# One-head attention: three fp16 passes for scores and values, turning two tiles behind, ScalarE's copies ahead of the exponential

## The chip, the cores and the metric

The kernel runs on one NeuronCore of a Trainium2 chip. Engines: TensorE (PE) with its weight loads (PEld), VectorE (DVE), ScalarE (ACT), GpSimd (POOL) and SyncE (SP). The metric is the time of one execution on the device in microseconds, the median of several runs.

## The reference

The whole program is a model of four layers, each of them an attention and a feed-forward part. The change touches the second branch of layer 0, a softmax attention with one head over x normalised, shape 4 x 1024 x 128, in fp32:

```python
q = x @ Wq + bq
k = x @ Wk + bk
v = x @ Wv + bv
scores = jnp.einsum('bqh,bkh->bqk', q, k) / sqrt(128)
attn = softmax(scores, axis=-1)
a = jnp.einsum('bqk,bkh->bqh', attn, v) @ Wo + bo
x = x + a
```

Its result goes into a softmax router and eight dense experts, the stages behind it. There are 4 batches of 1024 rows.

## The kernel before

`whole_attention` (L876) is called once, as stage `b0`; its tiles carry the prefix b_ in the profile. Data lie with the 128 features on the partitions. The work is cut into 32 tiles of 128 query rows, 8 per batch (`qts`); each tile's scores are 128 x 1024.

Five instruction streams are written out, one per engine, and every one walks the same list of jobs, `order`, made by `timeline()` (L884); semaphores join them. A step s of the list is: scores of tile s, turning of tile s-1, values of tile s-2; in the steps 4, 5 and 6 of a batch also k, q and v of the next batch; and every fourth step a projection with 512 columns. The jobs:

- k, q (L959): fp32 matmuls into one of the two wide PSUM buffers (`wide_ps`, 1024 columns each, shared with the scores). ScalarE adds k's bias (L1003), VectorE q's bias and scale (L1034).
- v (L966): eight fp32 matmuls into the PSUM tile `turned`, copied by ScalarE (L1014).
- scores (L974): two fp32 products with 512 columns into a wide buffer. VectorE takes the row maximum (L1042) and negates it (L1044), ScalarE makes exponential and row sum (L1008), VectorE the reciprocal (L1026) and scales the row (L1028), which is `normalise`.
- turn (L981): eight fp32 transposes of 128 x 128 of the scaled tile into `turned`, which has one buffer; ScalarE copies it to `prob_t` (L1019).
- values (L988): eight fp32 products of 128 columns into a quarter of `mix`. After four tiles VectorE adds v's bias (L1051, `mixed`).
- proj (L995): product with the output weights; VectorE adds bias and residual into `xp_t` (L1055), GpSimd adds that into `res_t` (L1063).

An fp32 product appears as two matmul records in the profile. VectorE runs `normalise(n - 1)` ahead of the row maximum of tile n. A wide buffer is refilled when its reader two slots before has freed it (`wait_freed`):

```python
if slot[job] >= 2:
    wait_freed(eng, wide[slot[job] - 2])
```

## Time and profile before

| | us |
|---|---|
| median of 3 runs | 4607.53 |
| lowest, highest run | 4606.55, 4609.24 |
| the profiled execution | 4609.92 |
| its span | 4608.0 |

Busy over the whole span:

| engine | busy us | share |
|---|---|---|
| PE | 4038.5 | 88% |
| PEld | 2252.7 | 49% |
| DVE | 3471.0 | 75% |
| ACT | 2976.9 | 65% |
| POOL | 2359.2 | 51% |

The profile is of one execution. Busy shares are means over stages that differ, so the stage of the change has to be looked at by itself. Matmuls are pipelined: a record's length is longer than the distance between two starts, and the distance is what it costs. The names "out<-in" are the program's tiles, and L numbers are lines of the kernel before.

### The profile page before, as it was taken

To read this page: it belongs to the slowest core of one execution; us is meant where nothing else is said; L and a number is where in the kernel's file an instruction comes from. 1 tells how busy PE (TensorE), PEld (TensorE's weight loads), DVE (VectorE), ACT (ScalarE), POOL (GpSimd) and SP (SyncE) were. 2 spreads that over 40 slices of the span, in tenths; PEclk is the share of its full clock that TensorE was granted. 3 is DMA by queue.
4 is the path that set the end of the run, shared out by engine and by line. 5 is a ranking of instruction groups with operands and counts; after the bars stand their busy time and mean duration, and the time that the engine had idled before them with its cause. 6 is when DMAs were issued, how large, how long until landed. Compare 5 with 4: busy or idle time off the path is not lost. (4 is left out here: it accounts for less than half of the span.)

```text
span 4608.0 us, 88475 instructions
## 1 busy us (share of the span) xinstructions
PE 4038.5 (88%) x34698; PEld 2252.7 (49%) x34700; DVE 3471.0 (75%) x4781; ACT 2976.9 (65%) x4498; POOL 2359.2 (51%) x1443
## 2 busy tenths in 40 slices
PE   6999999999998989976787778886888868999998
PEld 3666666666666644441121111434777443344443
DVE  6888888888884567756989897564777647988888
ACT  2777777777775469943767777672665725655555
POOL 2878887888883023320221110451666526666665
PEclk7999999999999989976989999997999979999999
DMA  2212221222110011100210100430000223333433
GB/s 81 57 43 53 57 55 45 51 57 57 45 41 1 1 70 69 46 5 25 81 62 27 39 26 6 128 125 19 13 13 14 100 91 98 88 101 99 99 96 87
DMA packets 112123, 261.46 MB, mean 57 GB/s; under 512 B 24020, under 2 KB 35668, under 8 KB 110236
## 3 DMA queue, kind: packets, MB, share of 16 engines
q1 hardware_dynamic: 96292, 215.01, 17.0%
q0 software_dynamic: 15424, 40.89, 2.6%
q8 instruction: 271, 4.44, 0.4%
q14 instruction: 136, 1.11, 0.1%
HBM read 170.31 MB, written 49.76 MB: 48 GB/s over the span
## 5 line engine op out<-in xcount | busy, mean ns | idle before, releaser
L522 POOL TENSOR_TENSOR a_prob_low<-a_prob_whole,a_prob_high 128x1024 f16<-128x1024 f32 x512 | 1084.4, 2131 | 277.2 <-ACT a_prob_high L412 275.4
L496 DVE TENSOR_REDUCE a_part_max<-a_top 128x2 f32<-128x1024 f32 x512 | 626.1, 1223 | 218.7 <-PE a_top L323 212.8
L409 ACT ACTIVATE a_prob_whole<-a_score 128x1024 f32<-128x1024 f32 x512 | 524.9, 1025 | 332.5 <-PE a_score L312 320.6
L767 ACT ACTIVATE a_prob<-a_score 128x512 f32<-128x512 f32 x1024 | 533.1, 604 | 259.3 <-PE a_score L711 259.2
L799 DVE TENSOR_REDUCE a_part_max<-a_side 128x2 f32<-128x1024 f32 x512 | 595.0, 1218 | 83.7 <-PE a_side L682 83.7
L1943 POOL TENSOR_TENSOR m_scaled<-m_acted,m_gate 128x512 f32<-128x512 f32 x264 | 433.3, 1650 | 269.4 <-DVE m_acted L2061 200.7
L412 ACT ACTIVATE a_prob_high<-a_score 128x1024 f16<-128x1024 f32 x512 | 522.3, 1020 | 0.0
L311 PE MATMUL a_score<-a_qa,a_ka 128*128 128x256 f16 x2048 | 476.3, 273 | 0.0
L312 PE MATMUL a_score<-a_qb,a_kb 128*128 128x256 f16 x2048 | 476.2, 273 | 0.0
L378 PE MATMUL a_o_ps<-a_v,a_prob_high 128*128 128x65 f16 x4096 | 428.1, 193 | 6.2 <-POOL a_prob_low L522 3.4
L380 PE MATMUL a_o_ps<-a_v,a_prob_high 128*128 128x64 f16 x4096 | 426.9, 194 | 0.0
L382 PE MATMUL a_o_ps<-a_v,a_prob_low 128*128 128x65 f16 x4096 | 424.5, 192 | 0.0
L378 PEld LDWEIGHTS a_o_ps<-a_v,a_prob_high 128*128 128x128 f16 x4096 | 376.0, 96 | 85.7 <-DVE a_tokens L482 35.3
L380 PEld LDWEIGHTS a_o_ps<-a_v,a_prob_high 128*128 128x128 f16 x4096 | 377.7, 97 | 26.9 <-issue 10.9
L382 PEld LDWEIGHTS a_o_ps<-a_v,a_prob_low 128*128 128x128 f16 x4096 | 377.9, 98 | 0.0
L1894 ACT ACTIVATE m_acted<-m_up_down 128x512 f32<-128x512 f32 x264 | 157.4, 597 | 319.4 <-PE m_up_down L1723 318.7
L711 PE MATMUL a_score<-a_qa,a_ka 32*128 32x512 f16 x1024 | 237.2, 398 | 91.0 <-ACT a_prob L767 88.6
L723 PE MATMUL a_o_ps<-a_prob,a_v 128*32 128x512 f32 x2048 | 285.9, 632 | 14.0 <-ACT a_raw L756 14.0
L2280 DVE TENSOR_TENSOR e_low<-e_whole,e_high 128x512 f16<-128x512 f32 x256 | 210.5, 833 | 82.7 <-ACT e_high L2238 82.1
L711 PEld LDWEIGHTS a_score<-a_qa,a_ka 32*128 32x128 f16 x1024 | 60.4, 92 | 431.1 <-ACT a_prob L767 366.6
L682 PE MATMUL a_side<-a_ka,a_qa 32*128 32x512 f16 x1024 | 217.4, 403 | 45.3 <-DVE a_part_max L799 22.6
L2067 DVE TENSOR_TENSOR m_lows<-m_scaled,m_high 128x512 f16<-128x512 f32 x264 | 241.8, 916 | 5.1 <-ACT m_high L1902 5.0
(439 smaller groups left out, 10380.4 us busy)
## 6 DMA issues: line engine op xcount, KB each, us to landing
m_gate<-gates SPq DMA_DIRECT2D x264, 256.0 KB
a_ka<-a_nat_high_k SPq DMA_DIRECT2D x128, 128.0 KB, 2.4
e_gate<-gates SPq DMA_DIRECT2D x8, 2048.0 KB, 7.2
slots<-in_slots SPq DMA_DIRECT2D x19, 520.0 KB, 4.1
a_qa<-a_nat_high_q SPq DMA_DIRECT2D x64, 128.0 KB, 2.4
a_qa<-a_nat_low_q SPq DMA_DIRECT2D x64, 128.0 KB, 2.4
a_qb<-a_nat_high_q SPq DMA_DIRECT2D x64, 128.0 KB, 2.4
a_kb<-a_nat_low_k SPq DMA_DIRECT2D x64, 128.0 KB, 2.4
```

Source lines behind the costliest of these rows:

```text
L311: eng.matmul(score[:, e % 2, h, i, :], ka[:, r, h, keys], qa[:, r, h, qs], start=True, stop=False)
L312: mm = eng.matmul(score[:, e % 2, h, i, :], kb[:, r, h, keys], qb[:, r, h, qs], start=False, stop=True)
L378: eng.matmul(o_ps[:, at:at + V1], high, v[:, r, kt, h, 0:V1], start=(pair == 0 and i == 0 and h == 0 and t == 0), stop=False, skip_group_c ...
L380: eng.matmul(o_ps[:, at:at + DH], high, v[:, r, kt, h, V1 + 1:VW], start=False, stop=False, skip_group_check=True)
L382: mm = eng.matmul(o_ps[:, at:at + V1], low, v[:, r, kt, h, 0:V1], start=False, stop=last, skip_group_check=True)
L409: eng.activation(prob_whole[:, e % RING, :, :, :], score[:, e % 2, :, :, :], ACT.Exp, scale=scale)
L412: eng.activation(prob_high[:, e % RING, :, :, :], score[:, e % 2, :, :, :], ACT.Exp, scale=scale).then_inc(exp_done, 1)
L496: eng.tensor_reduce(part_max[:, i, c, :, qt % 4], top[:, :, :], AX.X, ALU.max).then_inc(max_done, 1)
L522: eng.tensor_tensor(prob_low[:, e % RING, :, :, :], prob_whole[:, e % RING, :, :, :], prob_high[:, e % RING, :, :, :], ALU.subtract).then_ ...
L767: eng.activation(prob[:, e % RING, h, :], score[:, step % SLOTS, :], ACT.Exp).then_inc(exp_done, 1)
L799: op = eng.tensor_reduce(part_max[:, qt // 4, c, 2 * pair:2 * pair + 2, 24 + qt], side, AX.X, ALU.max)
L1943: eng.tensor_tensor(scaled[:, s % SR, :], acted[:, s % AR, :], gate[:, g % 2, j, c % 2 * BANK:(c % 2 + 1) * BANK], ALU.mult).then_inc(scal ...
```

## The change

1. k, q, v and the turned probabilities are each split in two fp16 parts: high is the value rounded to fp16, low the rest. Scores and values become three fp16 products (high x high, high x low, low x high), each with fp32 accumulation. The projections and the transposes stay fp32.
2. The high parts are made by ScalarE, the low parts of v and the turned tiles by VectorE (value in PSUM minus high), those of k and q by GpSimd. k and q are now first written in fp32 to one buffer each, then split.
3. `turned` is handled in two halves of 512 columns, each with waits of its own. Its fp16 parts are kept for four tiles side by side, so that values take 512 columns at once: the eight key tiles of a group of four query tiles are shared out over four value jobs, two each.
4. Turning runs two tiles behind the scores (before: one), values six (before: two, by tile), projections three steps later.
5. VectorE takes the row maximum of tile s, then the low parts of tile s-2, then scales tile s-1. ScalarE copies the high parts of tile s-2 ahead of the exponential of tile s.

The diff, cut:

```diff
+    HALF = qts // 2
...
-        for s in range(tiles + 3):
+        for s in range(tiles + 7):
             b, t = s // qts, s % qts
             if s < tiles:
                 order.append(("scores", s))
-            if 1 <= s < tiles + 1:
-                order.append(("turn", s - 1))
             if 2 <= s < tiles + 2:
-                order.append(("values", s - 2))
+                order.append(("turn", s - 2))
+            if 6 <= s < tiles + 6:
+                order.append(("values", s - 6))
             if b + 1 < B and t in (4, 5, 6):
                 order.append(("kqv"[t - 4], b + 1))
-            if s >= 3 and (s - 3) % 4 == 3:
-                order.append(("proj", (s - 3) // 4))
+            if s >= 10 and (s - 10) % 4 == 0:
+                order.append(("proj", (s - 10) // 4))
...
+    act_order = list(order)
+    for s in range(2, tiles):
+        i = act_order.index(("scores", s))
+        act_order[i:i + 2] = [("turn", s - 2), ("scores", s)]
...
-    turns = [job for job in order if job[0] in ("v", "turn")]
+    turns = [(*job, h) for job in order if job[0] in ("v", "turn") for h in range(2)]
...
-        q = pl.sb("q", [P, 2, N])
-        k = pl.sb("k", [P, 2, N])
-        v = pl.sb("v", [P, 2, qts, P])
+        q = pl.sb("q", [P, N])
+        k = pl.sb("k", [P, N])
+        q_high = pl.sb("q_high", [P, 2, N], F16)
+        q_low = pl.sb("q_low", [P, 2, N], F16)
+        k_high = pl.sb("k_high", [P, 2, N], F16)
+        k_low = pl.sb("k_low", [P, 2, N], F16)
+        v_high = pl.sb("v_high", [P, 2, qts, P], F16)
+        v_low = pl.sb("v_low", [P, 2, qts, P], F16)
...
-        prob_t = pl.sb("prob_t", [P, 2, N])
+        prob_high = pl.sb("prob_high", [P, 2, qts, BANK], F16)
+        prob_low = pl.sb("prob_low", [P, 2, qts, BANK], F16)
...
-        turned = pl.ps("turned", [P, N])
+        turned = pl.ps("turned", [P, 2, HALF, P])
...
+        def parts_of(what, n, h):
+            kts = slice(h * HALF, (h + 1) * HALF)
+            if what == "v":
+                return v_high[:, n % 2, kts, :], v_low[:, n % 2, kts, :]
+            at = slice(n % 4 * P, (n % 4 + 1) * P)
+            return prob_high[:, n // 4 % 2, kts, at], prob_low[:, n // 4 % 2, kts, at]
...
+                def product(dst, highs, lows, first, last):
+                    eng.matmul(dst, highs[0], highs[1], start=first, stop=False)
+                    eng.matmul(dst, highs[0], lows[1], start=False, stop=False)
+                    return eng.matmul(dst, lows[0], highs[1], start=False, stop=last)
...
+                    elif what in ("v", "turn"):
+                        if what == "turn":
+                            eng.wait_ge(prob_ready, n + 1)
+                        for h in range(2):
+                            i = turn[what, n, h]
+                            if i >= 2:
+                                eng.wait_ge(turned_read, i - 1)
+                            for t in range(HALF):
+                                kt = h * HALF + t
+                                if what == "v":
+                                    mm = eng.matmul(turned[:, h, t, :], xn_t[:, n * N + kt * P:n * N + (kt + 1) * P], w[:, 2, :], start=True, stop=True)
+                                else:
+                                    mm = eng.transpose(turned[:, h, t, :], prob[:, n % 3, kt * P:(kt + 1) * P], ident[:, :])
+                            mm.then_inc(turned_full, 1)
...
                         if t == 0:
-                            wait_freed(eng, ("k", b))
-                            wait_freed(eng, ("q", b))
+                            eng.wait_ge(qk_split, 2 * (b + 1))
+                        here = slice(t * P, (t + 1) * P)
                         for h in range(2):
-                            mm = eng.matmul(dst[:, h * BANK:(h + 1) * BANK], q[:, b % 2, t * P:(t + 1) * P],
-                                            k[:, b % 2, h * BANK:(h + 1) * BANK], start=True, stop=True)
+                            at = slice(h * BANK, (h + 1) * BANK)
+                            mm = product(dst[:, at], (q_high[:, b % 2, here], k_high[:, b % 2, at]), (q_low[:, b % 2, here], k_low[:, b % 2, at]), True, True)
...
                     elif what == "values":
-                        eng.wait_ge(turned_read, turn["turn", n] + 1)
-                        if n % 4 == 0 and n:
-                            eng.wait_ge(mixed_half, n // 4)
-                        for kt in range(qts):
-                            mm = eng.matmul(mix[:, t % 4 * P:(t % 4 + 1) * P], v[:, b % 2, kt, :], prob_t[:, n % 2, kt * P:(kt + 1) * P],
-                                            start=(kt == 0), stop=(kt == qts - 1))
-                        mm.then_inc(mixed_tile, 1)
+                        m, i = n // 4, n % 4
+                        if i == 0:
+                            eng.wait_ge(turned_read, turn["turn", 4 * m + 3, 1] + 1)
+                            if m:
+                                eng.wait_ge(mixed_half, m)
+                        for kt in (2 * i, 2 * i + 1):
+                            mm = product(mix[:, :], (v_high[:, b % 2, kt, :], prob_high[:, m % 2, kt, :]),
+                                         (v_low[:, b % 2, kt, :], prob_low[:, m % 2, kt, :]), kt == 0, kt == qts - 1)
+                        mm.then_inc(mixed_part, 1)
...
-                for job in by_act:
+                for job in act_order:
...
                     if what == "k":
                         eng.wait_ge(wide_full, slot[job] + 1)
-                        eng.activation(k[:, n % 2, :], wide_ps[:, slot[job] % 2, :], ACT.Identity, bias=bias[:, 1:2]).then_inc(act_freed, 1)
+                        if n:
+                            eng.wait_ge(qk_split, 2 * n - 1)
+                        eng.activation(k[:, :], wide_ps[:, slot[job] % 2, :], ACT.Identity, bias=bias[:, 1:2]).then_inc(act_freed, 1)
+                        wait_freed(eng, job)
+                        eng.activation(k_high[:, n % 2, :], k[:, :], ACT.Copy).then_inc(qk_high_done, 1)
+                    elif what == "q":
+                        wait_freed(eng, job)
+                        eng.activation(q_high[:, n % 2, :], q[:, :], ACT.Copy).then_inc(qk_high_done, 1)
...
                         if n >= 3:
-                            eng.wait_ge(turned_full, turn["turn", n - 3] + 1)
+                            eng.wait_ge(turned_full, turn["turn", n - 3, 1] + 1)
...
+                    elif what in ("v", "turn"):
+                        if what == "v" and n >= 2:
+                            eng.wait_ge(mixed_part, qts * (n - 1))
+                        if what == "turn" and n >= 8:
+                            eng.wait_ge(mixed_part, 4 * (n // 4 - 1))
+                        for h in range(2):
+                            eng.wait_ge(turned_full, turn[what, n, h] + 1)
+                            eng.activation(parts_of(what, n, h)[0], turned[:, h, :, :], ACT.Copy).then_inc(turned_high, 1)
...
                     if what == "q":
                         eng.wait_ge(wide_full, slot[job] + 1)
-                        eng.tensor_scalar(q[:, n % 2, :], wide_ps[:, slot[job] % 2, :], bias[:, 0:1], scale, ALU.add, ALU.mult).then_inc(dve_freed, 1)
+                        if n:
+                            eng.wait_ge(qk_split, 2 * n)
+                        eng.tensor_scalar(q[:, :], wide_ps[:, slot[job] % 2, :], bias[:, 0:1], scale, ALU.add, ALU.mult).then_inc(dve_freed, 1)
                     elif what == "scores":
-                        if n:
-                            normalise(n - 1)
                         eng.wait_ge(wide_full, slot[job] + 1)
                         at = slice(n % 4, n % 4 + 1)
                         if n >= 4:
-                            wait_freed(eng, ("scores", n - 4))
+                            eng.wait_ge(prob_ready, n - 3)
                         eng.tensor_reduce(top[:, at], wide_ps[:, slot[job] % 2, :], AX.X, ALU.max).then_inc(maxed, 1)
                         eng.wait_ge(maxed, n + 1)
                         eng.tensor_scalar(top[:, at], top[:, at], -1.0, None, ALU.mult).then_inc(negated, 1)
-                    elif what == "turn" and n == tiles - 1:
-                        normalise(n)
+                        if n == 1:
+                            normalise(0)
+                    elif what in ("v", "turn"):
+                        for h in range(2):
+                            i = turn[what, n, h]
+                            highs, lows = parts_of(what, n, h)
+                            eng.wait_ge(turned_high, i + 1)
+                            eng.tensor_tensor(lows, turned[:, h, :, :], highs, ALU.subtract).then_inc(turned_read, 1)
+                        if what == "turn" and n + 1 < tiles:
+                            normalise(n + 1)
...
-                for n in range(tiles // 4):
-                    at = slice(n * BANK, (n + 1) * BANK)
-                    eng.wait_ge(xp_done, n + 1)
-                    eng.tensor_tensor(res_t[:, at], res_t[:, at], xp_t[:, at], ALU.add).then_inc(res_done, 1)
+                splits = 0
+                for job in order:
+                    what, n = job
+                    if what in ("k", "q"):
+                        splits += 1
+                        whole, highs, lows = (k, k_high, k_low) if what == "k" else (q, q_high, q_low)
+                        eng.wait_ge(qk_high_done, splits)
+                        eng.tensor_tensor(lows[:, n % 2, :], whole[:, :], highs[:, n % 2, :], ALU.subtract).then_inc(qk_split, 1)
+                    elif what == "proj":
+                        at = slice(n * BANK, (n + 1) * BANK)
+                        eng.wait_ge(xp_done, n + 1)
+                        eng.tensor_tensor(res_t[:, at], res_t[:, at], xp_t[:, at], ALU.add).then_inc(res_done, 1)
```

**TensorE.** Rows of the order of instructions, in the middle of a batch; wide is the wide buffer, turned the transposed tile, mix the value sums. Before, from turning of one tile to the values of the next:

```order
L981 MATMUL b_turned<-all_kept_ident,b_prob 128x128 x8
L988 MATMUL b_mix<-b_prob_t,b_v 128x128 x8
L974 MATMUL b_wide<-b_k,b_q 128x512 x2
L981 MATMUL b_turned<-all_kept_ident,b_prob 128x128 x8
L988 MATMUL b_mix<-b_prob_t,b_v 128x128 x8
```

And now, from turning of one tile to the end of the next scores:

```order
L999 MATMUL b_turned<-all_kept_ident,b_prob 128x128 x8
L971 MATMUL b_mix<-b_prob_high,b_v_high 128x512
L972 MATMUL b_mix<-b_prob_low,b_v_high 128x512
L973 MATMUL b_mix<-b_prob_high,b_v_low 128x512
L971 MATMUL b_mix<-b_prob_high,b_v_high 128x512
L972 MATMUL b_mix<-b_prob_low,b_v_high 128x512
L973 MATMUL b_mix<-b_prob_high,b_v_low 128x512
L971 MATMUL b_wide<-b_k_high,b_q_high 128x512
L972 MATMUL b_wide<-b_k_low,b_q_high 128x512
L973 MATMUL b_wide<-b_k_high,b_q_low 128x512
```

The order of the kinds is the same; turning is that of a tile one older, and values are six products for a group of four tiles.

**VectorE**, the same place: maximum, negation, then scaling. Before:

```order
L1042 TENSOR_REDUCE b_top<-b_wide 128x1
L1044 TENSOR_SCALAR b_top<-b_top 128x1
L1026 RECIPROCAL b_total<-b_total 128x1
L1028 TENSOR_SCALAR b_prob<-b_prob,b_total 128x1024
L1042 TENSOR_REDUCE b_top<-b_wide 128x1
```

Now:

```order
L1075 TENSOR_REDUCE b_top<-b_wide 128x1
L1077 TENSOR_SCALAR b_top<-b_top 128x1
L1085 TENSOR_TENSOR b_prob_low<-b_turned,b_prob_high 128x4x128 x2
L1059 RECIPROCAL b_total<-b_total 128x1
L1061 TENSOR_SCALAR b_prob<-b_prob,b_total 128x1024
```

Two subtractions stand between the negation and the scaling, and the scaling is that of the tile before.

**ScalarE**, around k of the next batch. Before, each tile's exponential stands ahead of the copy of the tile before it:

```order
L1003 ACTIVATE b_k<-b_wide,all_kept_bias_b 128x1024
L1008 ACTIVATE b_prob,b_total<-b_wide,b_top 128x1024
L1019 ACTIVATE b_prob_t<-b_turned 128x1024
L1008 ACTIVATE b_prob,b_total<-b_wide,b_top 128x1024
L1019 ACTIVATE b_prob_t<-b_turned 128x1024
```

Now:

```order
L1033 ACTIVATE b_k<-b_wide,all_kept_bias_b 128x1024
L1035 ACTIVATE b_k_high<-b_k 128x1024
L1052 ACTIVATE b_prob_high<-b_turned 128x4x128 x2
L1043 ACTIVATE b_prob,b_total<-b_wide,b_top 128x1024
L1038 ACTIVATE b_q_high<-b_q 128x1024
L1052 ACTIVATE b_prob_high<-b_turned 128x4x128 x2
L1043 ACTIVATE b_prob,b_total<-b_wide,b_top 128x1024
```

The copies of tile s-2 stand ahead of the exponential of tile s, and the fp16 copies of k and q are new.

## Rows read from the trace of the kernel before

**Rows 1.** Busy time by stretch: stretch, length; busy (count) per engine; clock; DMA; GB/s.

```profile
1428.00:1460.00 32.00, 29.23 (x132) 18.38 (x133) 13.09 (x22) 12.93 (x17) 0.00 (x0) 0.89 0.01 1
1460.00:1600.00 140.00, 130.55 (x778) 94.36 (x777) 73.55 (x113) 57.08 (x78) 7.57 (x6) 1.00 0.00 1
```

**Rows 2.** Timeline of TensorE, a k step: start, length (us), engine, line, operation, count.

```profile
1503.19 1.88 PE L959 MATMUL b_wide<-all_xn_t,all_kept_w_b 128*128 128x512 f32 x4
1504.90 1.88 PE L974 MATMUL b_wide<-b_k,b_q 128*128 128x512 f32 x4
1506.62 1.04 PE L981 MATMUL b_turned<-all_kept_ident,b_prob 128*128 128x128 f32 x8
1507.49 1.95 PE L988 MATMUL b_mix<-b_prob_t,b_v 128*128 128x128 f32 x16
1509.28 1.02 PE L959 MATMUL b_wide<-all_xn_t,all_kept_w_b 128*128 128x512 f32 x2
```

**Rows 3.** Timeline of VectorE, one batch from row maximum to row maximum.

```profile
1506.82 1.22 DVE L1042 TENSOR_REDUCE b_top<-b_wide 128x1 f32<-128x1024 f32 x1 [2.46 <-PE b_wide L974]
1508.08 0.15 DVE L1044 TENSOR_SCALAR b_top<-b_top 128x1 f32<-128x1 f32 x1
...
1512.40 0.15 DVE L1026 RECIPROCAL b_total<-b_total 128x1 f32<-128x1 f32 x1
1512.59 0.75 DVE L1028 TENSOR_SCALAR b_prob<-b_prob,b_total 128x1024 f32<-128x1024 f32 x1
1513.26 1.22 DVE L1042 TENSOR_REDUCE b_top<-b_wide 128x1 f32<-128x1024 f32 x1
...
1553.07 1.23 DVE L1042 TENSOR_REDUCE b_top<-b_wide 128x1 f32<-128x1024 f32 x1 [2.46 <-PE b_wide L974]
```

**Rows 4.** Timeline of VectorE at the stage's start.

```profile
1433.99 1.28 DVE L1034 TENSOR_SCALAR b_q<-b_wide,all_kept_bias_b 128x1024 f32<-128x1024 f32 x1 [5.56 <-PE b_wide L959]
1437.49 1.22 DVE L1042 TENSOR_REDUCE b_top<-b_wide 128x1 f32<-128x1024 f32 x1 [2.22 <-PE b_wide L974]
```

**Rows 5.** Timeline of all engines, last tile and end of the stage.

```profile
1606.56 1.78 DVE L1028 TENSOR_SCALAR b_prob<-b_prob,b_total 128x1024 f32<-128x1024 f32 x1
1608.27 1.21 DVE L1042 TENSOR_REDUCE b_top<-b_wide 128x1 f32<-128x1024 f32 x1
1608.40 1.09 PE L981 MATMUL b_turned<-all_kept_ident,b_prob 128*128 128x128 f32 x8 [1.02 <-DVE b_prob L1028]
...
1616.65 0.75 DVE L1051 TENSOR_SCALAR b_mixed<-b_mix,all_kept_bias_b 128x512 f32<-128x512 f32 x1 [4.76 <-PE b_mix L988]
...
1619.45 1.26 POOL L1063 TENSOR_TENSOR all_res_t<-all_res_t,xp_t 128x512 f32<-128x512 f32 x1 [11.65 <-DVE xp_t L1055]
```

**Rows 6.** Timeline of TensorE in a later stage with fp16 matmuls.

```profile
1800.49 0.38 PE L2185 MATMUL e_out<-e_high,e_w_high 128*128 128x512 f16 x1
1800.70 0.38 PE L2186 MATMUL e_out<-e_low,e_w_high 128*128 128x512 f16 x1
```

**Rows 7.** Groups by line, other stages: shapes, count | busy us, mean ns | idle.

```profile
L441 DVE TENSOR_TENSOR a_nat_low_q<-a_side,a_nat_high_q 128x512 f16<-128x512 f32 x64 | 44.3, 692 | 2.2
...
L1894 ACT ACTIVATE m_acted<-m_up_down 128x512 f32<-128x512 f32 x264 | 157.4, 597 | 319.4 <-PE m_up_down L1723 318.7
L1888 ACT ACTIVATE m_x_high<-all_xn_t 128x1024 f16<-128x1024 f32 x4 | 4.1, 1046 | 0.0
...
L522 POOL TENSOR_TENSOR a_prob_low<-a_prob_whole,a_prob_high 128x1024 f16<-128x1024 f32 x512 | 1084.4, 2131 | 277.2 <-ACT a_prob_high L412 275.4 <-PE a_o_ps L382 1.8
```

**Rows 8.** Timeline of VectorE in an earlier stage, reads from PSUM.

```profile
131.79 0.69 DVE L469 TENSOR_TENSOR all_res_t<-all_res_t,a_side 128x512 f32<-128x512 f32 x1
132.44 0.16 DVE L478 TENSOR_SCALAR a_rec<-a_o_ps 128x4 f32<-128x4 f32 x1
```

**Rows 9.** Groups by line in this stage: exponential and scaling.

```profile
L1008 ACT ACTIVATE b_prob<-b_wide,b_top 128x1024 f32<-128x1024 f32 x32 | 35.6, 1113 | 92.9 <-DVE b_top L1044 92.9
...
L1028 DVE TENSOR_SCALAR b_prob<-b_prob,b_total 128x1024 f32<-128x1024 f32 x32 | 31.3, 979 | 1.1
```

More of the change, by code:

```diff
@@ L926, in whole_attention @@
         dve_freed = pl.sem("dve_freed")
+        qk_high_done = pl.sem("qk_high_done")
+        qk_split = pl.sem("qk_split")
         maxed = pl.sem("maxed")
@@ L931, in whole_attention @@
         turned_full = pl.sem("turned_full")
+        turned_high = pl.sem("turned_high")
         turned_read = pl.sem("turned_read")
-        mixed_tile = pl.sem("mixed_tile")
+        mixed_part = pl.sem("mixed_part")
         mixed_half = pl.sem("mixed_half")
@@ L961, in _ @@
                         mm.then_inc(wide_full, 1)
-                    elif what == "v":
-                        if turn[job]:
-                            eng.wait_ge(turned_read, turn[job])
-                        for t in range(qts):
-                            mm = eng.matmul(turned[:, t * P:(t + 1) * P], xn_t[:, n * N + t * P:n * N + (t + 1) * P], w[:, 2, :],
-                                            start=True, stop=True)
-                        mm.then_inc(turned_full, 1)
+                    elif what in ("v", "turn"):
[12 more added lines that the diff above has]
+                            mm.then_inc(turned_full, 1)
@@ L1044, in _ @@
                         eng.tensor_scalar(top[:, at], top[:, at], -1.0, None, ALU.mult).then_inc(negated, 1)
[L1045 to L1046 removed]
+                        if n == 1:
[8 more added lines that the diff above has]
+                            normalise(n + 1)
                     elif what == "values" and n % 4 == 3:
[L1048 removed]
+                        eng.wait_ge(mixed_part, n + 1)
                         if n >= 8:
```

18 lines of the change are left out of this document (removed).

## The prediction

> **What bounds the kernel now.** I read the granted clock and busy time by stretch first, to find the stage and its bound. The stage holds the time from 1428 to 1621 us, 193 of 4608 us. In its middle, 1460 to 1600 us, TensorE is busy 130.55 of 140 us at full clock (1.00, that is 2.4 GHz), VectorE 73.55, ScalarE 57.08, GpSimd 7.57 [rows 1]. So TensorE bounds it, and twice its slack lies in VectorE. Nothing before or behind the stage is touched, so every term below is a change of this stage's length.
>
> Next the timeline of TensorE, for what a tile costs there. The distances between first matmuls of neighbouring jobs say it: scores 1.72 us (1504.90 to 1506.62), turning 0.87 (to 1507.49), values 1.79 (to 1509.28), and a projection for k or q 1.72 (1503.19 to 1504.90) [rows 2]. A tile is 4.38 us. Then the timeline of VectorE, which gives the beat: I call T(s) the start of the row maximum of tile s. A batch is 8 tiles and takes 46.24 us (1506.82 to 1553.07) [rows 3]. TensorE's own work in it is 8 x 4.38 + 3 x 1.72 (k, q, v) + 2 x 0.86 (projections of half the columns of k) = 41.9; the other 4.3 us it waits. The whole: first row maximum 1437.49 [rows 4], last 1608.27, end of the last addition 1619.45 + 1.26 = 1620.71 [rows 5]. That is 170.78 us for 31 steps and 12.44 us of tail.
>
> **TensorE after the change.** Scores and values become 6 fp16 matmuls of 512 columns each per tile (values: 24 for four tiles). Such a matmul, with a weight load ahead of each one, starts every 0.215 us at full clock elsewhere in this program (1800.49, 1800.70) [rows 6]. So 1.29 + 0.87 + 1.29 = 3.45 us instead of 4.38. Turning stays fp32. Now a rule of another size: the Trainium skill's page "TensorE: Matmul & The Clock Gate", section Back-to-back issue gap, gives about 131 ns for a sustained matmul of 512 columns. By it these twelve would take 1.57 us and not 2.58; the rows say 215 ns and I take them.
>
> **VectorE after the change.** Added per tile are two subtractions (low part) of 512 columns, PSUM minus fp16 into fp16. The same operation takes 692 ns [rows 7], and an operation of that form lets the next one start after 0.65 us (131.79 to 132.44) [rows 8]. The row maximum holds the engine 1.26 us (1506.82 to 1508.08), the negation 0.15, the reciprocal 0.19 (1512.40 to 1512.59), the scaling 0.67 (to 1513.26) [rows 3]. Sum: 1.26 + 0.15 + 2 x 0.65 + 0.19 + 0.67 = 3.57 us.
>
> **ScalarE.** Its copy of 1024 becomes two of 512, 597 ns each from PSUM [rows 7], with the exponential of 1113 ns [rows 9]: 2.3 us per tile, and 0.1 for the sum it reads out. It is no bound, but it stands between the others. Turned half 0 is there at T(s) + 0.8, copied at T + 1.4, half 1 at T + 2.0. VectorE is through with maximum and negation at T + 1.41, so both subtractions run without waiting, and scaling of tile s-1 ends at T + 3.7. The exponential of s comes behind the copies and ends at T + 3.25.
>
> **The loop that sets the beat.** TensorE may turn tile s-1 only when it is scaled, at T(s) + 3.7. Behind it on TensorE stand values and then the scores of s+2. So: hand-over 0.14 (scaling lasts 0.08 longer than it holds VectorE, and turning starts 0.06 behind its end: 1606.56 + 1.78 to 1608.40 [rows 5]), turning 0.87, values 1.29, scores 1.29, and 0.2 from the next job's start to the row maximum (1506.62 to 1506.82 [rows 2, 3]): 3.79 us. That is a little more than VectorE's 3.57, so a plain tile takes 3.8 us and each engine waits a little for the other. I walked a batch with these durations:
> - tiles without extra work 3.8, then mixed (0.67 on VectorE) 4.3, then xp (0.67) 4.3, then 3.7;
> - the k tile 3.79 + 1.72 = 5.5, as all is on TensorE;
> - the q tile 5.8: VectorE has q (1.2) and mixed besides, ScalarE two fp16 copies of 1024, 1046 ns each [rows 7], and scores wait for an exponential of the tile before, since k and q take wide slots;
> - the v tile 6.6: v's halves wait for the subtractions of the turned tile, and the scores behind v and a projection for both;
> - the tile behind it 3.6.
> Together 37.6 us against 46.24 now. In the first batch no values run until tile 6, and two tiles run without subtractions: 30.6. The last has no k, q, v: 28.4 for 7 steps. T(0) to T(31): 30.6 + 2 x 37.6 + 28.4 = 134.2.
>
> **GpSimd.** Eight subtractions of 1024 are new, 2131 ns each [rows 7]. Two are at the start (below). For the other six see what GpSimd does to the scaling: beside an addition of 1.26 us it takes 1.78 us, not 0.75 (1606.56) [rows 5]; over all 32 tiles its mean is 979 ns [rows 9], 7.2 us in all. Those eight additions now start beside the row maximum and are over before the scaling comes, so that this loss goes (it is in the 46.24, not in my walk). A subtraction for k or q meets a scaling (0.75 in some 5 us) only in part: bounds 0 and 6 x 2.13 = 12.8 us; in the walk both only touch one, so I take 1.5, near the lower end. The Trainium skill's page "SBUF — State Buffer", section SBUF: two separate sides, speaks against this part: VectorE and GpSimd share a port pair, whoever starts first holds it for the whole instruction, and the other blocks. By it every meeting would cost up to the rest of 2.13 us. The 1.78 us fit that.
>
> **Start.** Scores of tile 0 now need split k and q. VectorE's q starts at 1433.99 and ends at 1435.3 [rows 4]; copy to fp16 1.05, GpSimd 2.13 behind k's own, which is done by then, so with hand-overs the first scores start at 1438.8 and take 1.3 + 0.2: T(0) = 1440.3 at full clock, 1441.6 at half, against 1437.49 [rows 4]. I take +3.5 us. TensorE stands some 3 us longer there, and the clock of the first 32 us is 0.89 now [rows 1]; for more of that I add 1.5 us (bounds 0 and 6: three tiles' scores and turnings at half clock).
>
> **Tail.** Turning lags two tiles and values six. From T(31): scaling of 30 done at 3.7, turned, copied, subtracted at 6.3; scaling of 31 done at 7.2, turned 8.1, subtracted 9.8, mixed of the group before 10.6, then 24 matmuls 5.2 + 0.2, and mixed to the last addition 4.06 as now (1616.65 to 1620.71) [rows 5]: 20.1 us against 12.44, +7.7.
>
> **Sum.** Steps: 134.2 + 1.5 + 1.5 = 137.2 against 170.8, -33.6. Start +3.5, tail +7.7. Net -22.4 us. The profiled execution took 4609.92, so 4587.5; it was 2.4 us above the median of the three runs, 4607.53, so at the median's level **4585**.
>
> **Rivals.** A measurement tells about 0.2% (9.2 us) from no change.
> - *Meetings and waits eat half.* All six subtractions on GpSimd hold the scaling for their whole length (12.8 instead of 1.5): gain 11.1, 4596. For: the 1.78 us. Against: the meeting is short in my walk. If the cold start costs its 6 us as well: gain 6.6, 4601, no change that can be told.
> - *More.* TensorE is quicker than 0.215 us per matmul, or hands over sooner, and VectorE's 3.57 sets the plain tiles. 20 of the 31 steps are plain: -0.23 each, and 2 us less in k, q, v tiles and tail: gain 29, 4579. This is also what the page's 131 ns would make of it. Against: rows 6.
> - *Slower: the two wide slots.* On ScalarE the exponential of s is now behind two copies that wait for TensorE's turning, and TensorE may not start scores s+2 before it ends. It ends at T + 3.25, the slot is wanted at T + 5.9. If copies or their waits took 2.6 us more (two copies of 1.9 and not 0.6), every tile would lose what is over, and the lookahead with it: a beat of exponential, scores and hand-over, 3.25 + 1.5 = 4.75 us. 31 x 0.95 = 29 us more: 4614. It decides from there. The k and q tiles show a bit of it already.
>
> **Chances.** Forecast 0.68 (4580 to 4592), first rival 0.12 at 4596 and 0.07 at 4601, more 0.09, slower 0.04. Faster by over 0.2%: 0.68 + 0.12 + 0.09 less a little for 4596 being near the line: 0.87. Within 0.2%: 0.09. Slower: 0.04. The range 4577 to 4597 leaves out the 4601 and the slower case.
>
> **What would show it.** In the profile after: row maxima of plain tiles 3.8 us apart, batches some 37.6; fp16 matmuls every 0.215 us; subtractions 0.69; VectorE over 85% busy in the middle of the stage; a few row maxima waiting for scores by 0.2, scalings near 0.75 with at most six longer; first row maximum about 3.5 us later; tail 20. It is wrong if turning waits for ScalarE or VectorE for more than half a microsecond in plain tiles, if scores wait for an exponential outside of k, q and v, or if the clock stays at half.

## The result, and the profile after

The changed kernel took 4575.06 us (median of 4 runs, 4571.28 to 4576.66) against 4608.01 us of the kernel before run beside it; the ratio is 0.9927, 95% interval 0.991 to 0.9945. That is 33 us less. The forecast was 4585 and faster, with a range down to 4577: the direction is right, the gain was set a third too low, and the time lies 2 us below the range.

The stage of the change can be measured by itself, from q's bias on VectorE (the start of the first such instruction) to the end of GpSimd's last addition. It took 186.72 us before and 158.17 now, 28.55 less. The rest of the two profiled spans differs by 6.4 us (4421.3 against 4414.9); more on that below.

Busy time by stretch of the stage after the change (columns as in [rows 1]):

```profile
1460.00:1560.00 100.00, 97.62 (x529) 56.20 (x527) 90.99 (x155) 60.23 (x104) 17.00 (x10) 1.00 0.00 1
```

Against [rows 1] VectorE went from half busy to 90.99 of 100 us, and TensorE, at 97.62, works almost without a gap at the full clock. Two engines are now full where one was.

Groups by line in the stage (shapes, count | busy us, mean ns | idle us before, and who ended it):

```profile
L1085 DVE TENSOR_TENSOR b_prob_low<-b_turned,b_prob_high 128x512 f16<-128x512 f32 x64 | 41.1, 684 | 4.0 <-ACT b_prob_high L1052 3.7
L1075 DVE TENSOR_REDUCE b_top<-b_wide 128x1 f32<-128x1024 f32 x32 | 39.1, 1222 | 10.0 <-PE b_wide L973 10.0
L1043 ACT ACTIVATE b_prob<-b_wide,b_top 128x1024 f32<-128x1024 f32 x32 | 35.8, 1117 | 6.6 <-DVE b_top L1077 6.1
L1052 ACT ACTIVATE b_prob_high<-b_turned 128x512 f16<-128x512 f32 x64 | 34.6, 592 | 41.4 <-PE b_turned L999 41.4
L971 PE MATMUL b_wide<-b_k_high,b_q_high 128*128 128x512 f16 x64 | 25.0, 391 | 4.7 <-POOL b_q_low L1108 3.2 <-ACT b_prob L1043 1.4
L1061 DVE TENSOR_SCALAR b_prob<-b_prob,b_total 128x1024 f32<-128x1024 f32 x32 | 24.6, 768 | 1.1
L1108 POOL TENSOR_TENSOR b_q_low<-b_q,b_q_high 128x1024 f16<-128x1024 f32 x4 | 8.5, 2128 | 10.1 <-ACT b_q_high L1038 10.1
```

The new operations cost what [rows 7] gave: 684 ns for a subtraction (692), 592 for a copy (597), 2128 on GpSimd (2131). The scaling fell from a mean of 979 to 768 ns, since GpSimd's additions no longer stand beside it. ScalarE hardly idles before the exponential any more, 6.6 us in all against 92.9 in [rows 9]; it now idles before the copies that stand ahead of it, 41.4 us.

Timeline of VectorE over three row maxima in the plain part of a batch (the counterpart of [rows 3]):

```profile
1502.61 1.23 DVE L1075 TENSOR_REDUCE b_top<-b_wide 128x1 f32<-128x1024 f32 x1 [0.17 <-PE b_wide L973]
1503.87 0.15 DVE L1077 TENSOR_SCALAR b_top<-b_top 128x1 f32<-128x1 f32 x1
1503.94 1.28 DVE L1085 TENSOR_TENSOR b_prob_low<-b_turned,b_prob_high 128x512 f16<-128x512 f32 x2
1505.13 0.15 DVE L1059 RECIPROCAL b_total<-b_total 128x1 f32<-128x1 f32 x1
1505.33 0.75 DVE L1061 TENSOR_SCALAR b_prob<-b_prob,b_total 128x1024 f32<-128x1024 f32 x1
1506.07 1.23 DVE L1075 TENSOR_REDUCE b_top<-b_wide 128x1 f32<-128x1024 f32 x1
1507.33 0.15 DVE L1077 TENSOR_SCALAR b_top<-b_top 128x1 f32<-128x1 f32 x1
1507.52 1.29 DVE L1085 TENSOR_TENSOR b_prob_low<-b_turned,b_prob_high 128x512 f16<-128x512 f32 x2
...
1509.85 1.22 DVE L1075 TENSOR_REDUCE b_top<-b_wide 128x1 f32<-128x1024 f32 x1 [0.19 <-PE b_wide L973]
```

TensorE in the second of these tiles, turning (of the tile just scaled), scores and their end:

```profile
1506.13 1.09 PE L999 MATMUL b_turned<-all_kept_ident,b_prob 128*128 128x128 f32 x8
...
1508.36 0.38 PE L971 MATMUL b_wide<-b_k_high,b_q_high 128*128 128x512 f16 x1
...
1509.44 0.38 PE L973 MATMUL b_wide<-b_k_high,b_q_low 128*128 128x512 f16 x1
```

One tile takes 3.46 us, the next 3.78, together 7.24. The last maximum waited 0.19 us for the scores. The chain behind it can be read from these rows: from the first maximum to the end of the scaling 3.47 us (1502.61 to 1505.33 + 0.75 = 1506.08), then turning 0.05 later, values, scores, and the maximum two steps on at 1509.85, 3.77 us behind the scaling. A whole batch, from maximum 13 to 21, takes 36.42 us (46.25 before). In order its tiles take 5.44 (q), 6.68 (v), 3.46, 3.78, 4.05 (mixed), 4.05 (xp), 3.46 and 5.50 (k).

Start and tail, timelines of TensorE and GpSimd:

```profile
1437.35 0.58 PE L971 MATMUL b_wide<-b_k_high,b_q_high 128*128 128x512 f16 x1 [3.17 <-POOL b_q_low L1108]
1437.72 0.63 PE L972 MATMUL b_wide<-b_k_low,b_q_high 128*128 128x512 f16 x1
...
1440.61 0.38 PE L973 MATMUL b_wide<-b_k_high,b_q_low 128*128 128x512 f16 x1
```

```profile
1589.34 1.26 POOL L1112 TENSOR_TENSOR all_res_t<-all_res_t,xp_t 128x512 f32<-128x512 f32 x1 [4.59 <-DVE xp_t L1096]
```

The first scores waited 3.17 us for q's low part, and then started every 0.43 us until 1440.3; the granted clock from 1437.35 to 1440.30 was 0.50, the lower level (1.2 GHz). The first maximum is 7.67 us behind q's bias (3.50 before). From the last maximum, 1569.72, to the last addition's end at 1590.60 there are 20.88 us (12.44 before). In the list of jobs the projections run four steps later than before (s = 10 instead of 6 for the first), not three.

### The profile page after: what moved, and what is told of

Same layout as the page of the kernel before. It is cut to its first block and busy times, and to the rows that moved or that the text cites. A ratio compares the mean times of both kernels' runs of the same rounds, so it can differ in the third digit from the quotient of the medians.

```text
span 4573.1 us, 88090 instructions
## 1 busy us (share of the span) xinstructions
PE 4009.7 (88%) x34442; PEld 2207.9 (48%) x34444; DVE 3509.2 (77%) x4853; ACT 2992.3 (65%) x4542; POOL 2381.8 (52%) x1451
## 5 line engine op out<-in xcount | busy, mean ns | idle before, releaser
L522 POOL TENSOR_TENSOR a_prob_low<-a_prob_whole,a_prob_high 128x1024 f16<-128x1024 f32 x512 | 1085.2, 2131 | 276.6 <-ACT a_prob_high L412 276.5
L378 PEld LDWEIGHTS a_o_ps<-a_v,a_prob_high 128*128 128x128 f16 x4096 | 376.4, 96 | 85.8 <-DVE a_tokens L482 35.4
```

The lines of the kernel that those rows point to most:

```text
L378: eng.matmul(o_ps[:, at:at + V1], high, v[:, r, kt, h, 0:V1], start=(pair == 0 and i == 0 and h == 0 and t == 0), stop=False, skip_group_c ...
L522: eng.tensor_tensor(prob_low[:, e % RING, :, :, :], prob_whole[:, e % RING, :, :, :], prob_high[:, e % RING, :, :, :], ALU.subtract).then_ ...
```

## The experiments

Twelve runs. Since the rest of the program varies by itself, they are compared by the stage: from q's bias to the end of the last addition, and by the batch from maximum 13 to 21, both from the profiled execution. Theory A is that the beat comes from a loop over VectorE and TensorE in which both the lag and ScalarE's order are needed; the rivals are named with each.

| run | stage us | batch us | median us | ratio to the kernel before, interval |
|---|---|---|---|---|
| before | 186.72 | 46.25 | 4608.01 | |
| the change | 158.17 | 36.42 | 4575.06 | 0.9927, 0.991 to 0.9945 |
| e1_exp_first | 214.13 | 51.36 | 4626.91 | 1.0052, 1.0035 to 1.0069 |
| e2_lag_one | 176.56 | 40.97 | 4590.15 | 0.9964, 0.995 to 0.9979 |
| e3_fp32_lag_two | 179.45 | 43.96 | 4598.47 | 0.9983, 0.9972 to 0.9995 |
| e10_fp32_copy_first | 170.36 | 41.97 | 4586.59 | 0.9976, 0.9962 to 0.9991 |
| e4_two_passes | 155.68 | 36.04 | 4578.42, one run | |
| e5_short_low | 152.42 | 35.47 | 4565.15, one run | |
| e6_both_short | 147.19 | 34.07 | 4561.31, one run | |
| e8_edges | 154.00 | 36.42 | 4569.68 | 0.9927, 0.9911 to 0.9944 |
| e9_edges_mixed | 153.12 | 36.07 | 4568.18 | 0.9928, 0.9911 to 0.9944 |
| e11_edges_spread | 154.68 | 36.16 | 4562.62 | 0.9931, 0.9916 to 0.9946 |
| e12_change_again | 158.19 | 36.42 | 4563.74 | 0.9944, 0.993 to 0.9957 |
| e13_before_again | 185.99 | 46.24 | 4591.27, one run | |

The kernel before ran beside the others too: 4606.6 us with e1 to e3, 4603.65 with e8 and e9, 4593.19 with e10 to e12.

### ScalarE's order undone

```diff
-    for s in range(2, tiles):
-        i = act_order.index(("scores", s))
-        act_order[i:i + 2] = [("turn", s - 2), ("scores", s)]
```

> ScalarE makes the exponential of tile s before the two high copies of tile s-2, all else as in the change. Theory A (the copies feed VectorE's subtractions, so their place decides): exponential from T+1.44 to T+2.68, copies to 3.25 and 3.8, subtractions to 4.5, scaling to 5.3, so a plain tile takes about 5.3 us instead of 3.6, a batch some 49 us instead of 36.4, the whole about 4625 us, slower than the kernel before. Rival (ScalarE is busy 60% only, so its order does not matter): batch 36.4, 4575 us.

Stage 214.13 us, batch 51.36, slower than the kernel before. VectorE's timeline in a plain tile:

```profile
1476.33 1.22 DVE L1072 TENSOR_REDUCE b_top<-b_wide 128x1 f32<-128x1024 f32 x1
1477.59 0.15 DVE L1074 TENSOR_SCALAR b_top<-b_top 128x1 f32<-128x1 f32 x1
1479.50 1.29 DVE L1082 TENSOR_TENSOR b_prob_low<-b_turned,b_prob_high 128x512 f16<-128x512 f32 x2 [1.76 <-ACT b_prob_high L1049]
1480.70 0.15 DVE L1056 RECIPROCAL b_total<-b_total 128x1 f32<-128x1 f32 x1
1480.89 0.75 DVE L1058 TENSOR_SCALAR b_prob<-b_prob,b_total 128x1024 f32<-128x1024 f32 x1
1481.56 1.22 DVE L1072 TENSOR_REDUCE b_top<-b_wide 128x1 f32<-128x1024 f32 x1
```

The maximum-to-maximum distance is 5.23 us, and 1.76 of it is a wait of the subtractions for ScalarE's copy. Theory A said 5.3 for a plain tile and 49 for the batch, which took 51.36. ScalarE has time enough in total; what counts is that VectorE's queue stands still until its copies are there. With the exponential in front, split and lag together make the stage 27.4 us longer than that of the kernel before.

### Turning one tile behind

```diff
-            if 2 <= s < tiles + 2:
-                order.append(("turn", s - 2))
+            if 1 <= s < tiles + 1:
+                order.append(("turn", s - 1))
...
-                        if n == 1:
+                        if n == 0:
                             normalise(0)
```

ScalarE's list is changed in the same way (copies of s-1 ahead of the exponential of s).

> Turning runs one tile behind the scores instead of two, copies still ahead of the exponential. Theory A (scaling of tile s then waits for the exponential of the same tile, which ends at T+3.25): step of VectorE 3.25 + 0.2 + 0.7 = 4.15 us, mixed and xp tiles 4.8, batch 41 us instead of 36.4, about 4594 us. Rival (VectorE's work of 3.46 sets the beat wherever turning stands): batch 36.4, 4575 us.

Stage 176.56, batch 40.97: theory A's sum of 41 is met, its parts are not. The plain tiles take 3.57 and 3.97, and the load sits in the mixed tile, 6.31:

```profile
1518.99 1.22 DVE L1075 TENSOR_REDUCE b_top<-b_wide 128x1 f32<-128x1024 f32 x1
1520.24 0.15 DVE L1077 TENSOR_SCALAR b_top<-b_top 128x1 f32<-128x1 f32 x1
1522.19 1.29 DVE L1085 TENSOR_TENSOR b_prob_low<-b_turned,b_prob_high 128x512 f16<-128x512 f32 x2 [1.79 <-ACT b_prob_high L1052]
```

There the subtractions wait 1.79 us for the copy. By the list of waits ScalarE's copies waited 16.4 us in six cases behind values on TensorE: a group of four tiles may only be overwritten when its values are through, and with turning one step nearer that becomes a wait. So the lag is worth 18.4 us of stage, a part of it through this second wait, which the expectation did not have; how large a part was not taken apart.

### The order without the split

The kernel before, fp32 throughout, turning two tiles behind and values three:

```diff
-            if 1 <= s < tiles + 1:
-                order.append(("turn", s - 1))
-            if 2 <= s < tiles + 2:
-                order.append(("values", s - 2))
+            if 2 <= s < tiles + 2:
+                order.append(("turn", s - 2))
+            if 3 <= s < tiles + 3:
+                order.append(("values", s - 3))
```

> The kernel before in fp32, with turning two tiles behind and values three: the order alone, without the split. Theory A (before, TensorE's 41.9 us of work per batch plus waits that the lag removes): batch 42.0 to 42.5 instead of 46.25, tail about 3 us longer, about 4595 to 4598 us. Rival (the waits come from the wide buffers and GpSimd, not the lag): batch 46, 4610 us.

Stage 179.45, batch 43.96, between the 42.0 to 42.5 of theory A and the 46 of the rival. The v tile kept a wait (timeline of TensorE):

```profile
1513.81 2.05 PE L966 MATMUL b_turned<-all_kept_w_b,all_xn_t 128*128 128x128 f32 x16 [1.33 <-ACT b_prob_t L1019]
```

1.33 us for a copy that stands behind the exponential on ScalarE. So the copies were put first here too:

```diff
+    for s in range(2, tiles):
+        i = by_act.index(("scores", s))
+        by_act[i:i + 2] = [("turn", s - 2), ("scores", s)]
```

> The fp32 kernel with turning two tiles behind, and now ScalarE's copy of tile s-2 ahead of the exponential of tile s: all of the new order, none of the split. Theory A (the lag-two run's batch of 43.96 us still held a wait of 1.33 us of v for the copy behind the exponential): batch 42.0 to 42.6, that is TensorE's own work of 41.9, about 4592 us. The other theory (only the split makes the order worth anything): batch 44.

Stage 170.36, batch 41.97, TensorE without any gap (by stretch):

```profile
1460.00:1580.00 120.00, 120.00 (x731) 89.40 (x730) 70.40 (x110) 54.73 (x74) 7.62 (x6) 1.00 0.00 1
```

That is the 41.9 us of TensorE's own work in the prediction, to 0.1. With this the change comes apart: the new order alone takes 16.4 us off the stage (186.72 to 170.36), 7.3 by the lag and 9.1 by the copies put first, and the rest another 12.2 (to 158.17). The rest is the split with what goes with it, the halves of `turned` and the values of four tiles together; these were not tried one by one. With the exponential first, the same step costs 34.7 us (179.45 to 214.13).

### What bounds a tile: one engine, or the loop

Three runs cut the work of one engine or both. First scores without the pass of q's low part times k's high part (left out of the computation), 0.43 us less on TensorE:

```diff
-                            mm = product(dst[:, at], (q_high[:, b % 2, here], k_high[:, b % 2, at]), (q_low[:, b % 2, here], k_low[:, b % 2, at]), True, True)
+                            eng.matmul(dst[:, at], q_high[:, b % 2, here], k_high[:, b % 2, at], start=True, stop=False)
+                            mm = eng.matmul(dst[:, at], q_high[:, b % 2, here], k_low[:, b % 2, at], start=False, stop=True)
```

> Scores in two passes: low part of q times high part of k is left out, 0.43 us less on TensorE per tile. Theory A (a loop over two steps, 3.6 on VectorE to the scaled tile and 3.65 on TensorE to the scores two steps on, 7.25 for two tiles, bounded below by 2 x 3.46 on VectorE): the 3.77 tile becomes 3.46, k tile 5.49 to 5.06, v tile 6.68 to 6.25, batch 36.43 to 35.3. Rival B (VectorE alone bounds): batch stays 36.4. Rival C (TensorE alone bounds): 8 x 0.43 less, 33.0.

Then 0.40 us less on VectorE, the low part of three quarters of each second half left out (GpSimd sets it to zero once, at the start):

```diff
-                            eng.tensor_tensor(lows, turned[:, h, :, :], highs, ALU.subtract).then_inc(turned_read, 1)
+                            if what == "turn" and h == 1:
...
+                                eng.tensor_tensor(lows[:, 0:1, :], turned[:, h, 0:1, :], highs[:, 0:1, :], ALU.subtract).then_inc(turned_read, 1)
+                            else:
+                                eng.tensor_tensor(lows, turned[:, h, :, :], highs, ALU.subtract).then_inc(turned_read, 1)
...
+                eng.memset(prob_low[:, :, 5:8, :], 0.0).then_inc(cleared_low, 1)
```

> The subtraction of half 1 of each turned tile takes 128 columns instead of 512 (the rest of the low part is zero), 0.40 us less on VectorE per tile. Theory A (loop over two steps): the 3.77 tile to 3.45 (TensorE's work), mixed and xp tiles 4.05 to 3.66, k tile as it is, q 5.44 to 5.2, v 6.68 to 6.5, batch 36.43 to 34.7. Rival B (VectorE alone bounds): 8 x 0.4 less, 33.2. Rival C (TensorE alone bounds): 36.4.

> Both cuts at once: scores without the pass of q's low part, and the short subtraction. Theory A: cuts add up where each engine held the other, plain tiles about 3.2, batch 33.3 or less. Rivals B and C: no more than the better of the two cuts alone.

Batches 36.04, 35.47 and 34.07, where theory A said 35.3, 34.7 and at most 33.3. For the first cut alone VectorE's rival (36.4) was nearer than theory A; the second gave 1.0 us, where the rivals said 3.2 or nothing, and both cuts together give 1.4 us more than the better one, which neither rival allows. VectorE's timeline with both cuts, from one maximum to the second next:

```profile
1500.37 1.21 DVE L1077 TENSOR_REDUCE b_top<-b_wide 128x1 f32<-128x1024 f32 x1
...
1502.67 0.75 DVE L1063 TENSOR_SCALAR b_prob<-b_prob,b_total 128x1024 f32<-128x1024 f32 x1
...
1506.77 1.23 DVE L1077 TENSOR_REDUCE b_top<-b_wide 128x1 f32<-128x1024 f32 x1 [0.16 <-PE b_wide L1009]
```

To the end of the scaling 3.05 us (0.42 less than in the change), from there to the maximum two steps on 3.35 (0.42 less), 6.40 for two tiles: the loop over two steps got shorter by both cuts.

With two passes alone each batch fell by 0.4 us and not by 1.1: the mixed tile took 4.24 and the q tile 5.87 instead of 4.05 and 5.44. The trace shows why. There is a third loop, over one step, that theory A did not have: turning, ScalarE's copy, the subtractions, the next scaling. In the run with two passes:

```profile
1504.02 1.09 PE L999 MATMUL b_turned<-all_kept_ident,b_prob 128*128 128x128 f32 x8 [0.69 <-DVE b_prob L1062]
1504.77 1.09 ACT L1053 ACTIVATE b_prob_high<-b_turned 128x512 f16<-128x512 f32 x2 [1.63 <-PE b_turned L999]
...
1505.40 1.29 DVE L1086 TENSOR_TENSOR b_prob_low<-b_turned,b_prob_high 128x512 f16<-128x512 f32 x2
```

The scaling before them ends at 1503.96, the next at 1506.80 + 0.75 = 1507.55: 3.59 us. The subtractions start 0.27 us behind the negation (0.07 where the copy is there in time), as the copy ends at 1505.37. In the change the same loop took 3.58 (1506.08 to 1509.66), against 3.62 for the mean plain tile; so shorter scores alone could bring little. In the q tile the copies stand behind k's on ScalarE, and the subtractions waited 0.45 us where they waited 0.1 in the change. VectorE's timeline of the run with two passes, a tile earlier:

```profile
1500.51 1.21 DVE L1076 TENSOR_REDUCE b_top<-b_wide 128x1 f32<-128x1024 f32 x1
1501.75 0.15 DVE L1078 TENSOR_SCALAR b_top<-b_top 128x1 f32<-128x1 f32 x1
1501.82 1.28 DVE L1086 TENSOR_TENSOR b_prob_low<-b_turned,b_prob_high 128x512 f16<-128x512 f32 x2
1503.02 0.15 DVE L1060 RECIPROCAL b_total<-b_total 128x1 f32<-128x1 f32 x1
1503.21 0.75 DVE L1062 TENSOR_SCALAR b_prob<-b_prob,b_total 128x1024 f32<-128x1024 f32 x1
1503.88 1.22 DVE L1076 TENSOR_REDUCE b_top<-b_wide 128x1 f32<-128x1024 f32 x1
```

Here nothing waits: 3.37 us is VectorE's own time for a plain tile. In the run with the short subtraction the maxima of plain tiles, two in a row here, wait for TensorE instead:

```profile
1506.39 1.22 DVE L1076 TENSOR_REDUCE b_top<-b_wide 128x1 f32<-128x1024 f32 x1 [0.40 <-PE b_wide L974]
...
1509.85 1.22 DVE L1076 TENSOR_REDUCE b_top<-b_wide 128x1 f32<-128x1024 f32 x1 [0.40 <-PE b_wide L974]
```

and the distance is 3.46, TensorE's own 3.45. So the change's 3.46 tiles are TensorE's bound, and the 3.78 tiles are the rest of the loop over two steps.

### The two ends

```diff
+                        if n == 0:
+                            eng.wait_ge(qk_high_done, 2)
+                            for h in range(2):
+                                eng.matmul(dst[:, h * BANK:(h + 1) * BANK], q_high[:, 0, 0:P], k_high[:, 0, h * BANK:(h + 1) * BANK], start=True, stop=False)
...
+                        if n == 0:
+                            eng.wait_ge(dve_freed, 1)
+                            eng.wait_ge(qk_high_done, 2)
+                            eng.tensor_tensor(q_low[:, 0, :], q[:, :], q_high[:, 0, :], ALU.subtract).then_inc(qk_split, 1)
...
-                        if what == "turn" and n + 1 < tiles:
+                        if what == "turn" and n + 2 < tiles:
                             normalise(n + 1)
+                        if what == "turn" and n + 3 == tiles:
+                            normalise(n + 2)
```

> Only the two ends of the stage: q's low part of the first batch made by VectorE, the first scores begin with the high passes before the low parts are there; the last tile is scaled right behind the one before it. Theory A (start and tail stand on the path in full): first row maximum 1 to 1.5 us earlier counted from q's bias on VectorE (7.67 us now), tail 1.8 us shorter (20.9 us from the last row maximum now), together about 3 us, 4572 us. Rival (clock and waits eat it): no change.

The batch is the same, the start 4.90 instead of 7.67 us, the tail 19.48 instead of 20.88 (1.4 less, where 1.8 was expected), the stage 154.00. The start gave 2.8 us where 1 to 1.5 was expected:

```profile
1433.74 0.59 PE L1005 MATMUL b_wide<-b_k_high,b_q_high 128*128 128x512 f16 x2 [0.77 <-ACT b_q_high L1046]
1435.05 0.39 PE L1012 MATMUL b_wide<-b_k_low,b_q_high 128*128 128x512 f16 x1 [0.72 <-DVE b_q_low L1081]
1435.28 0.38 PE L1013 MATMUL b_wide<-b_k_high,b_q_low 128*128 128x512 f16 x1
```

The two standstills were 0.77 and 0.72 us instead of one of 3.17, and the matmuls behind them came every 0.22 us; the granted clock from 1433.7 to 1438 was 1.00.

### Two tries at the middle

ScalarE adds v's bias (mixed) in place of VectorE, on top of the ends:

```diff
-                        eng.tensor_scalar(mixed[:, n // 4 % 2, :], mix[:, :], bias[:, 2:3], None, ALU.add).then_inc(mixed_half, 1)
...
+                        eng.activation(mixed[:, n // 4 % 2, :], mix[:, :], ACT.Identity, bias=bias[:, 2:3]).then_inc(mixed_half, 1)
```

> The ends as in the run before, and v's bias for the group of four tiles (mixed) added by ScalarE instead of VectorE. Theory A (the mixed tiles are bound by VectorE at 4.05 us): those tiles 3.5 to 3.6, q tiles 5.44 to about 5.2, batch 36.43 to 35.6, 3 us over the stage, together with the ends about 6 us less than the change, 4569 us. Rival (ScalarE's exponential behind it comes late and scores wait for it): batch 36.4 or more.

Stage 153.12. The mixed tile fell from 4.05 to 3.58 and the xp tile behind it rose from 4.05 to 4.52; the two together stayed at 8.10. That is the loop over two steps with the projection in it, 3.47 + 3.77 + 0.86 = 8.10: taking 0.67 us from VectorE could not shorten the two together, and the second maximum now waits for TensorE:

```profile
1478.66 1.22 DVE L1092 TENSOR_REDUCE b_top<-b_wide 128x1 f32<-128x1024 f32 x1 [0.39 <-PE b_wide L973]
```

0.9 us of the 3 expected are left, from the q and v tiles.

Then, on top of the ends alone, k, q and v of the next batch in steps 1, 4 and 7:

```diff
-            if b + 1 < B and t in (4, 5, 6):
-                order.append(("kqv"[t - 4], b + 1))
+            if b + 1 < B and t in (1, 4, 7):
+                order.append(("kqv"[t // 3], b + 1))
```

> As the run on the ends, with k, q and v of the next batch in steps 1, 4 and 7 instead of 4, 5 and 6: k beside mixed (VectorE's load beside TensorE's), q and v apart from mixed and projection. Theory A (a tile costs the larger of TensorE's and VectorE's sums): batch 35.4 to 35.7 instead of 36.42, stage from q's bias to its end 151.5 instead of 154.0, about 4567 us. Rival (each of k, q, v costs the lookahead of the wide slots wherever it stands): batch 36.4.

Batch 36.16 and stage 154.68, no better than the ends alone. k beside mixed took 5.50 us, as expected, but q in a plain tile took 5.50 as well: a k or q job costs a tile TensorE's chain of 5.5 us behind the scaling (3.77 + 1.72) wherever it stands, so the rival (batch 36.4) is nearer to the measured 36.16 than theory A (35.4 to 35.7).

### The same kernels again

> The changed kernel unaltered, on another occasion. Stage from q's bias to its end 158.2 us again to within 0.5. If the rest of the program varies by itself, the time outside the stage differs from 4414.9 us by some us; if it is fixed, by less than 1.

> The kernel before unaltered, on another occasion. Stage 186.7 us again; outside it 4421.3 us if the rest is fixed, and anywhere between 4407 and 4421 us if it varies as in the other runs.

The change's stage is 158.19, the same to 0.02 us. The stage of the kernel before is 185.99, 0.7 shorter than the first time, all of it among the first four tiles. But the span outside the stage was 4403.7 us for the change and 4403.3 for the kernel before (spans 4561.9 and 4589.3), where it was 4414.9 and 4421.3. Over all profiled executions it lies between 4403 and 4421.

## Why the prediction was right or wrong

- **TensorE bounded it, VectorE was next.** Right. The fp16 matmuls came every 0.215 us (0.22 by the timeline), as in [rows 6], and not 0.131 as the Trainium skill's page "TensorE: Matmul & The Clock Gate", section Back-to-back issue gap, has for a sustained stream: the trace disagrees with that figure.
- **The loop that sets the beat: this step failed.** It was put as 3.79 us per tile: scaling, turning, values, scores, maximum. The links are right and so is their length, 3.77 measured. But they lead from the scaling in step s to the maximum of step s+2. So they bound two tiles together: 3.47 from T(s) to the end of the scaling, 3.77 to T(s+2), 7.24 in all. With the prediction's own 3.7 and 3.79 that would have been 7.49 for two plain tiles, where two beats of 3.8 make 7.6. The plain tiles are 3.46 (TensorE's work) and 3.78, where the walk had 3.6 to 3.8.
- **VectorE's sum, 3.57 us, was too large: the term that was mis-sized.** The run with two passes shows 3.37: two subtractions one behind the other hold the engine 1.20 us, not 1.30 (1501.82 to 1503.02), and the negation 0.07, not 0.15. This made mixed and xp tiles 4.05, where 4.3 was forecast, the q tile 5.44 instead of 5.8, and it is also the larger part of the 7.6 - 7.24 above (3.7 against 3.47).
- **Both together** made the walk too long by 1.0 us in the first batch, 1.2 in each of the next two and 1.2 in the last: 134.2 us were forecast and 129.62 measured, 4.6 less. In a middle batch 0.5 of it are the mixed and xp tiles, 0.4 the q tile and 0.4 the two tiles of 3.46; the v tile took 0.1 more than forecast.
- **Meetings with GpSimd, 1.5 us.** Five scalings of 32 were longer, by 0.1 each, 0.5 in all. GpSimd's additions moved off the scaling, as forecast. Of two operations that need the port pair shared by VectorE and GpSimd, the Trainium skill's page "SBUF — State Buffer", section SBUF: two separate sides, has the later blocked until the first is through; the trace agrees for this scaling, whose end follows GpSimd's by the same time in both cases. Before the change, the last scaling of [rows 5] ran beside this addition on GpSimd and ended 0.55 us behind its end (1606.56 + 1.78 against 1606.53 + 1.26):

```profile
1606.53 1.26 POOL L1063 TENSOR_TENSOR all_res_t<-all_res_t,xp_t 128x512 f32<-128x512 f32 x1 [18.56 <-DVE xp_t L1055]
```

After it, the scaling at 1463.46 also ends 0.55 behind GpSimd's subtraction (1464.30 against 1463.75), but met only its end and lost 0.09 instead of 1.03:

```profile
1461.62 2.13 POOL L1108 TENSOR_TENSOR b_q_low<-b_q,b_q_high 128x1024 f16<-128x1024 f32 x1 [3.01 <-ACT b_q_high L1038]
```

```profile
1463.46 0.84 DVE L1061 TENSOR_SCALAR b_prob<-b_prob,b_total 128x1024 f32<-128x1024 f32 x1
```

- **Clock in the first tiles, 1.5 us.** Apart from the first scores, which the start has, it cost nothing to be seen: with the ends changed, where those scores ran at full clock, the 31 steps took 129.62 us as well. With the point above some 2.5 to 3 us were added for next to nothing: steps 129.62 us where 137.2 were forecast, 7.6 less.
- **Start.** +4.2 us where 3.5 was taken between 2.8 at full and 4.1 at half clock: it was half clock, and the 4.1 had it right. **Tail:** +8.4 instead of 7.7.
- So the stage lost 41.2 - 4.2 - 8.4 = 28.6 us where 33.6 - 3.5 - 7.7 = 22.4 was forecast.
- **Nothing outside the stage changes: true of the program, not of one measurement.** The other stages differ by up to 18 us between executions of the same kernels. The 33 us of the first comparison are 28.6 of the stage and some 4.4 of this. That the median fell below the range is due to this part: taken from 4607.53, a gain of 28.6 gives 4579, inside it. The prediction put this term at nothing because nothing there is touched. Side by side later the medians differed by 29.4 us.
- **The rivals.** The slower one, lookahead lost to copies that end too late, did not happen, but the run with the exponential first shows that it was near: one exponential (1.1 us and its sum) ahead of the copies is enough. The rival "more" had the right size, gain 29, which is luck: it rested on quicker matmuls or on VectorE's 3.57 as the beat, and the matmuls came every 0.215 us and VectorE needed 3.37.
- **A reading.** "Twice its slack lies in VectorE" should be seven times: TensorE was idle 9.45 of 140 us, VectorE 66.45 [rows 1].

## What to carry to other kernels

Where one engine's queue holds both a short job that the next engine waits for and a long one with slack, the short one goes first; here that order is worth 56 us of a 158 us stage, though the engine is 60% busy. When a chain leads from one step to the step after next, write it as a bound on two steps, not on one. When one engine's work gets shorter, look for the next loop first: here one of 3.58 us stood right below the 3.62 of the mean tile. And measure a change of 0.6% in its own stage, since the rest of a long program can vary by more than it gains.

## What was not expected of the hardware

- Times outside the stage varied from 4403 to 4421 us over 14 profiled executions with the same instructions there. It is not spread over the program. Counted from the stage's end, three stretches hold most of it (positions as in the kernel before): 1960 to 2100 us took 135.9 to 140.6 us, 2850 to 3250 took 390.5 to 407.5, and 3560 to 3800 took 232.7 to 240.5, and the time up to q's bias was 1431.2 to 1436.2, while 2100 to 2850 took 749.3 to 751.0 in all but one execution (755.8). What differs inside them stays open.
- TensorE ran at half clock (granted clock 0.50) for 3 us after standing 3.17 us at the start, and at full clock after two standstills of 0.77 and 0.72 us. From the first scores to the first maximum it took 2.75 us, where full clock would have made it some 1.5 (an estimate, six matmuls of 0.215 us and 0.2): the wait cost 1.25 us more than its length.
- Two VectorE subtractions of 512 columns in a row take 1.20 us between their first start and the next instruction, 0.60 each, though one alone is shown with 0.68 to 0.69.
